# One row statistic of a state-space block, moved from GpSimd to ScalarE (Trainium2, one core)

## What is computed

```
def _layernorm(x, axis=-1, eps=1e-05):
    m = jnp.mean(x, axis=axis, keepdims=True)
    v = jnp.var(x, axis=axis, keepdims=True)
    return (x - m) / jnp.sqrt(v + eps)
...
    xz = einsum(hidden, in_proj_w);  x, z = halves of xz
    x_conv = silu(sum of 4 shifted x * conv_w + conv_b)
    dt_in, Bv, Cv = parts of einsum(x_conv, x_proj_w)
    delta = softplus(einsum(dt_in, dt_proj_w) + dt_proj_b)
    h = h * exp(d_t * A) + (d_t * u_t) * B_t;  y = sum over n of h * C_t
    y = (y + x_conv * D) * silu(z);  out = einsum(y, out_proj_w)
...
    x = x + _L0_attn_ref(_layernorm(x, axis=-1), ...)
    x = x + _L0_ffn_ref(_layernorm(x, axis=-1), ...)
```

## Time and profile before

| | |
|---|---|
| median of 3 runs | 6447.79 us (6447.11 to 6450.78) |
| the profiled execution, its own time | 6448.49 us |
| span of its profile | 6446.7 us |
| TensorE busy | 6085.9 us, 94% |
| GpSimd (POOL) busy | 5053.7 us, 78% |
| VectorE (DVE) busy | 4238.7 us, 66% |
| ScalarE (ACT) busy | 3553.7 us, 55% |
| granted TensorE clock, mean | 0.978 |

### The profile page before, as it was taken

One profiled execution on the slowest core, in us unless ns is written; L12 is line 12 of the kernel. 1 busy time (PEld: TensorE's weight loads), 2 busy tenths in 40 slices (PEclk: granted clock), 3 DMA queues, 4 the chain that ended last, 5 costly groups with the idle time before them and its releaser, 6 DMA issues. The chain is left out here.

```text
span 6446.7 us, 78759 instructions
## 1 busy us (share of the span) xinstructions
PE 6085.9 (94%) x25311; PEld 3902.1 (61%) x25312; DVE 4238.7 (66%) x5700; ACT 3553.7 (55%) x6456; POOL 5053.7 (78%) x3844
## 2 busy tenths in 40 slices
PE   7999999999999999999998699996999999999999
PEld 3444444444444444444443488885888888888887
DVE  6999999999999999999999567787000000000000
ACT  5677676767676776777676478873222222222221
POOL 6999999999999999999999687762445555554554
PEclk9999999999999999999999999998999999999999
DMA  3545554555555555555544334443666666666554
GB/s 122 165 164 170 165 171 162 164 168 168 165 164 172 165 166 166 170 162 165 170 166 161 99 100 124 124 128 72 180 183 181 189 185 180 189 186 179 178 169 123
DMA packets 562603, 1028.78 MB, mean 160 GB/s; under 512 B 90578, under 2 KB 256980, under 8 KB 527632
## 3 DMA queue, kind: packets, MB, share of 16 engines
q1 hardware_dynamic: 455088, 668.00, 32.6%
q0 software_dynamic: 107104, 355.74, 18.7%
HBM read 925.79 MB, written 88.08 MB: 157 GB/s over the span
## 5 line engine op out<-in xcount | busy, mean ns | idle before, releaser
L365 POOL TENSOR_TENSOR m_dbu<-m_du,m_bb 128x1024 f32<-128x1024 f32 x1024 | 2398.7, 2381 | 0.0
L743 PE MATMUL m_y_bank<-m_prod,m_ident 128*128 128x512 f32 x4096 | 1976.8, 612 | 147.3 <-POOL m_prod L374 147.3
L516 ACT ACTIVATE m_decay<-m_delta,m_a_neg 128x512 f32<-128x512 f32 x2048 | 1419.4, 695 | 725.7 <-DVE m_h L626 723.8
L743 PEld LDWEIGHTS m_y_bank<-m_prod,m_ident 128*128 128x128 f32 x4096 | 788.8, 196 | 1126.7 <-issue 907.5
L1795 DVE TENSOR_SCALAR e_ye<-e_ybank,e_share 128x256 f32<-128x256 f32 x270 | 118.2, 479 | 1768.3 <-PE e_ybank L1828 1768.3
L626 DVE TENSOR_TENSOR_SCAN m_h<-m_decay,m_h_end,m_dbu 128x512 f32<-128x512 f32 x1024 | 1258.5, 1265 | 3.6 <-ACT m_decay L516 2.5
L626 DVE TENSOR_TENSOR_SCAN m_h<-m_decay,m_dbu 128x512 f32<-128x512 f32 x1024 | 1196.2, 1204 | 12.6 <-ACT m_decay L516 12.0
L1776 ACT ACTIVATE e_a<-e_ubank 128x512 f32<-128x512 f32 x540 | 322.5, 597 | 1473.4 <-PE e_ubank L1819 1472.2
L374 POOL TENSOR_TENSOR m_prod<-m_h,m_cb 128x1024 f32<-128x1024 f32 x416 | 989.6, 2379 | 18.1 <-issue 13.7
L1819 PE MATMUL e_ubank<-e_xT,s_w 128*128 128x256 f32 x4320 | 978.4, 380 | 1.3 <-ACT e_xT L1767 1.3
L1828 PE MATMUL e_ybank<-s_w,e_a 128*128 128x256 f32 x4320 | 954.5, 379 | 0.7 <-ACT e_a L1776 0.7
(11 more groups left out here) (213 smaller groups left out, 6506.5 us busy)
## 6 DMA issues: line engine op xcount, KB each, us to landing
m_bb<-rows_bc SPq DMA_DIRECT2D x1024, 256.0 KB, 3.6
m_cv<-rows_bc SPq DMA_DIRECT2D x608, 256.0 KB, 3.8
m_cb<-rows_bc SPq DMA_DIRECT2D x416, 256.0 KB, 3.3
m_xin<-in_x SPq DMA_DIRECT2D x32, 512.0 KB, 5.6
m_xres<-in_x SPq DMA_DIRECT2D x32, 512.0 KB, 5.4
x<-m_xres SPq DMA_DIRECT2D x32, 512.0 KB, 6.0
a_xa<-x SPq DMA_DIRECT2D x64, 256.0 KB, 2.8
a_xr<-x SPq DMA_DIRECT2D x64, 256.0 KB, 3.2
```

Of the source, the lines that this page charges most:

```text
L365: nc.gpsimd.tensor_tensor(dbu[:, slot], du[:, q[1], p * PC:(p + 1) * PC], bb[:, slot].unsqueeze(1).to_broadcast([P, PC, T]), ALU.mult).the ...
L516: nc.scalar.activation(decay[:, cc], delta[:, r, c], ACT.Exp, scale=a_neg[:, c, n:n + 1]).then_inc(decay_done, 1)
L743: ins = nc.tensor.matmul(y_bank[:, cc], ident[:], prod[:, slot, cc], start=False, stop=(n == NS - 1))
```

## The change

GpSimd's four instructions and the two constants they read go. ScalarE gets a function of the same name with seven instructions: Ln of variance plus eps, Exp of minus half of that (the same inverse deviation), a multiplication by -1, and four one-column activations for -mean * rstd. The first three of them are each followed by a wait for their result. They are issued at v = 47, after the Exp of the second step-size group, and once ahead of the first block, where the table for Exp and Ln is loaded for them.

```
-            def inverse_deviation(q):
-                wait(pool, stats_done, count(q, 2, 2))
-                wait(pool, ln_done, count(q, 1, 0))
-                nc.gpsimd.tensor_tensor(rstd[:], moments[:, :, 1], eps[:], ALU.add).then_inc(rstd_done, 1)
-                nc.gpsimd.tensor_tensor(shift[:], moments[:, :, 0], minus_one[:], ALU.mult).then_inc(rstd_done, 1)
-                wait(pool, rstd_done, count(q, 4, 2))
-                nc.gpsimd.tensor_tensor(rstd[:], rstd[:], minus_half[:], ALU.pow).then_inc(rstd_done, 1)
-                wait(pool, rstd_done, count(q, 4, 3))
-                nc.gpsimd.tensor_tensor(shift[:], shift[:], rstd[:], ALU.mult).then_inc(rstd_done, 1)
...
-            inverse_deviation((0, 0))
-            inverse_deviation((0, 1))
...
-                        if u == STATS_AT // PC + 2 and not last:
-                            inverse_deviation(after(after(q)))
...
+            def inverse_deviation(q):
+
+                wait(act, stats_done, count(q, 2, 2))
+                wait(act, ln_done, count(q, 1, 0))
+                nc.scalar.activation(rstd[:], moments[:, :, 1], ACT.Ln, bias=eps[:, 0:1]).then_inc(rstd_done, 1)
+                wait(act, rstd_done, count(q, 4, 1))
+                nc.scalar.activation(rstd[:], rstd[:], ACT.Exp, scale=-0.5).then_inc(rstd_done, 1)
+                wait(act, rstd_done, count(q, 4, 2))
+                nc.scalar.mul(minus_rstd[:], rstd[:], -1.0).then_inc(rstd_done, 1)
+                wait(act, rstd_done, count(q, 4, 3))
+                for j in range(TB):
+                    ins = nc.scalar.activation(shift[:, j:j + 1], moments[:, j, 0:1], ACT.Identity,
+                                               scale=minus_rstd[:, j:j + 1])
+                ins.then_inc(rstd_done, 1)
...
+                if v == DEVIATE_AT and norm:
+                    inverse_deviation(after(q))
                 if v - NORMALISE_AT in (0, 1) and norm:
                     normalise(after(q), v - NORMALISE_AT)
...
+            nc.scalar.preload_act_table_set("natural_log_exp_and_others")
+            inverse_deviation((0, 0))
             normalise((0, 0), 0)
```

More of the change, by code:

```diff
@@ L104, in mamba_stage @@
     NORMALISE_AT = STATS_AT + 8
+    DEVIATE_AT = NORMALISE_AT - 2
     STORE_ROWS_AT = (position_of["dbl", 0] + 2 + TAKE) // PC
@@ L152, in mamba_stage @@
         shift = sb("shift", [P, TB])
-        minus_half = sb("minus_half", [P, TB])
-        minus_one = sb("minus_one", [P, TB])
+        minus_rstd = sb("minus_rstd", [P, TB])
         eps = sb("eps", [P, TB])
@@ L293, in _ @@
                 sp.dma_start(dst, src).then_inc(s_weights, 16)
-            sp.wait_ge(s_const, 5)
+            sp.wait_ge(s_const, 3)
             w_xT = w["x_T"].rearrange("(c p) e -> p c e", p=P)
@@ L334, in _ @@
         def _(pool):
-            nc.gpsimd.memset(minus_half[:], -0.5).then_inc(s_const, 1)
-            nc.gpsimd.memset(minus_one[:], -1.0).then_inc(s_const, 1)
             nc.gpsimd.memset(eps[:], EPS).then_inc(s_const, 1)
@@ L339, in _ @@
             nc.gpsimd.memset(w_x[:], 0.0).then_inc(s_const, 1)
-            pool.wait_ge(s_const, 5)
+            pool.wait_ge(s_const, 3)
             nc.gpsimd.affine_select(out=ident[:], in_=ident[:], compare_op=ALU.not_equal, fill=1.0,
                                     base=0, pattern=[[-1, P]], channel_multiplier=1).then_inc(s_const, 1)
-            def inverse_deviation(q):
-                wait(pool, stats_done, count(q, 2, 2))
-                wait(pool, ln_done, count(q, 1, 0))
-                nc.gpsimd.tensor_tensor(rstd[:], moments[:, :, 1], eps[:], ALU.add).then_inc(rstd_done, 1)
-                nc.gpsimd.tensor_tensor(shift[:], moments[:, :, 0], minus_one[:], ALU.mult).then_inc(rstd_done, 1)
-                wait(pool, rstd_done, count(q, 4, 2))
-                nc.gpsimd.tensor_tensor(rstd[:], rstd[:], minus_half[:], ALU.pow).then_inc(rstd_done, 1)
-                wait(pool, rstd_done, count(q, 4, 3))
-                nc.gpsimd.tensor_tensor(shift[:], shift[:], rstd[:], ALU.mult).then_inc(rstd_done, 1)
             def du_part(q, part):
@@ L406, in _ @@
             act.wait_ge(s_weights, 16 * 9)
-            act.wait_ge(s_const, 6)
+            act.wait_ge(s_const, 4)
             nc.scalar.activation(a_neg[:], a_log[:], ACT.Exp).then_inc(s_a, 1)
@@ L533, in _ @@
             dve.wait_ge(s_weights, 16 * 9)
-            dve.wait_ge(s_const, 6)
+            dve.wait_ge(s_const, 4)
             for c in range(CH):
@@ L657, in _ @@
             pe.wait_ge(s_a, 4)
-            pe.wait_ge(s_const, 6)
+            pe.wait_ge(s_const, 4)
             pe.wait_ge(s_weights, 16 * 9)
```

## The result

| | before | after |
|---|---|---|
| median | 6449.28 us (4 runs, 6447.11 to 6453.02) | 6498.8 us (4 runs, 6494.77 to 6506.6) |
| span of the profile | 6446.7 us | 6493.0 us |
| granted TensorE clock, mean | 0.978 | 0.974 |

The ratio is 1.0077, 95% interval 1.0065 to 1.0089: slower by 50 us, where 6457 us (between 6432 and 6478) had been forecast. The time went up by more than five times the forecast 9.6 us.

A forecast was written before the change was run, and what follows sets the result against it. GpSimd was taken as the bound, with VectorE close behind. The profiled 6448.5 us, plus 9.0 for 15 pairs and 0.6 at the start, gave 6458.1, stated as 6457 us against the runs' median; range 6432 to 6478 us.

The forecast's parts named there:

- What bounds the kernel: State-space stage: GpSimd, 99.4% busy, holds VectorE back by at most 1.12 us in one block and 1.36 in the other.
- The chain on ScalarE: Seven new instructions at v = 47: 1.6 us together, between 1.1 and 2.3 us.
- The dearer chain: Rival: ScalarE's seven instructions cost more than their pieces, deciding from about 1.7 us; 6478 us at 2.3 us; chance 0.21.
- the extra table load: Rival: a table load beside ScalarE's seven instructions in every block, 1.28 us x 30; excluded by the order of instructions.
- How late VectorE gets: Scans waiting for the decays of v = 48 and 50: VectorE 1.3 us late in even blocks, 1.55 in odd.
- the swap: GpSimd's four instructions against ScalarE's seven: one wait nearly replaces another, +0.18 us even block, +0.42 odd, +0.60 a pair.
- The second part of `m_du`: Odd block: GpSimd waits about 2 us for the last delta and starts 0.42 us later, delaying the gate by +0.42 us.
- A pair grows by 0.60 us, 15 pairs by 9.0 us: Sum over the loop: even block +0.18 us and odd block +0.42 us, times 15 pairs.
- TensorE's queue starts there from the gate. That wait moves with the gate and gives nothing back.: VectorE's 1.29 us wait after a gate, for ScalarE's C copy behind TensorE's fill: no gain from a shorter GpSimd.
- The start of the program: Ahead of the first block: +0.6 us from ScalarE's second preparation; two added table loads taken as costing 0.
- the signs that would show the prediction wrong: Profile after: small new waits for decays (faster), ScalarE's seven instructions over 1.8 us (slower), or unchanged waits at the gates.
- GpSimd's saving goes through: Rival: ScalarE delays no scan, so GpSimd's relief saves 37 us, to 6411 us; chance of a gain over 0.2%: 0.17.

## Why the prediction was wrong

- **What bounds the kernel.** Right in kind and in sum. "By no more" than 1.12 and 1.36 us a block does GpSimd hold VectorE back: that made 37 us for its four instructions. At full clock they cost 41 us, and the pair 2.45 us (221.15 - 218.70) against 2.48. That the sums agree so closely is in part luck, since the parts do not: at full clock the waits are 1.83 us in the even block and 0.31 in the odd. The 1.36 us of the odd block stood behind matmuls at the lower clock (3.45 us for four). Rows 3 also left out three waits of that pair, 0.34, 1.40 and 0.33 us; all three stand unchanged in the changed kernel, so nothing hangs on them.
- **The chain on ScalarE.** Right in length, 1.56 against 1.6 us. The dearer chain and the extra table load are out.
- **How late VectorE gets.** Even block 1.3 us forecast, 2.57 measured, but 0.98 at full clock. Odd block 1.55 forecast; 0.17 + 1.35 + 0.16 = 1.68 measured, but 0.15 at full clock, so that the forecast came near there by luck. Both sums rested on decays that the trace of before showed with little in hand. The odd block's were late there already (0.17 us), and at full clock that wait is gone: the four matmuls behind that block's v = 36 gate took 3.2 us in the trace of before and 1.98 with spare matmuls. The sign of the swap was wrong by this too: it was put at +0.60 us a pair and is -1.0.
- **The second part of `m_du`.** It was to start 0.42 us later from the gate; it starts 0.50 us later (36.60 against 36.10 us behind the gate at v = 36). GpSimd waits there for the last delta, as described, but 1.11, not 2 us, because it waits 1.09, 0.30 and 0.60 us ahead of its products before that. This agreement is luck as well: with the clock held, the multiplication starts 1.25 us *earlier* behind that gate than in the kernel before (34.90 against 36.15 us; its wait is 0.32 us), so the odd block's +0.42 us is no part of the swap.
- **The step that failed** is the sum "A pair grows by 0.60 us, 15 pairs by 9.0 us": it has no term for TensorE's own speed, and gives no reason for leaving it out. It goes back to "TensorE's queue starts there from the gate. That wait moves with the gate and gives nothing back." The wait itself did just that, and is still 1.29 us. But that step, and every sum behind it, took what TensorE does from the gates on as it stood in the trace: same matmuls, same durations, same distance to the fills that ScalarE takes. The matmuls took 3.67 for 1.98 us and 4.01 for 2.74, and ScalarE's fill came 1.7 us later. That was worth +4.4 us a pair, where my whole sum was +0.60.
- The rows were there to doubt it. In the earlier trace rows four matmuls take 3.45 us behind a wait of 2.97 us, where the same four take 1.88 us elsewhere in that trace (1032.00). I read the row for the wait and not for the duration beside it.
- **The start of the program.** The first matmuls behind a v = 4 gate start 1.2 us later (83.60 against 82.36), where 0.6 was put. The two added table loads cost nothing, as taken: ScalarE still waits 2.98 us for the statistics behind the first and 1.55 us for TensorE behind the second.
- **The rivals and the signs.** None was this one, and of the signs that would show the prediction wrong none came: the waits for decays were not small, the chain was not over 1.8 us, and the gates' waits shrank. The gain of "GpSimd's saving goes through" is real at full clock (no chain: 41 us below), but with the clock left to itself even the kernel without any chain won only 8 us.

The Trainium skill (TensorE: Matmul & The Clock Gate, What's actually happening) says that the low clock is the default and that activity releases it. The runs agree: spare matmuls in the waits bring the stage from 0.97 to 1.00.

What stays open is why a given wait loses the clock and another of the same length does not. The runs show that it depends on what lies around it (one covered wait changes the clock behind another), and no run here isolates more than that. Some 5.5 us of the 46.3 us between the spans lie outside the 15 pairs, 1.2 ahead of them and 4.3 behind, and were not followed up.

## What to carry to other kernels

When an engine that is nearly always busy has short waits, read the duration of the matmuls behind each wait and the granted clock there before costing anything: a change on other engines that moves those waits can move the clock, and it outweighed the change's own terms here by four to one. To judge a change by its own merit, compare both versions with spare matmuls in TensorE's waits. And if they bring the time down, keep them: they were worth 73 to 77 us to one version and 10 to the other. Then look again for the place of the moved work: two positions earlier it cost nothing here.

## What the hardware showed that I had not expected

- The same wait of 1.44 us ahead of the same matmuls keeps the clock in one pair of blocks (1.98 us at 580.67) and loses it in the next (3.65 us at 804.23), in one execution, and from then on in every pair to the last (3.65 to 3.68 us). In the kernel before it is the other way round: the first pair takes 3.67 us behind that wait (at 135.67), all later ones 1.98.
- Lengths of a pair gather at one value when the clock is not held: 221.88 us before, and in the profiled executions (each the slowest of ten) 221.86 without any chain and 221.87 with the chain at v = 45; 221.87 also in the changed kernel with spare matmuls at unit 1 alone. At full clock the first two differ by 2.45 us. In the kernel without any chain the saving was lost again behind waits at the lower clock; why the lengths meet at this value no run shows.
- More work was faster, twice: four more activations on ScalarE by 20 us, five spare matmuls a block on TensorE by 77 us.
- On ScalarE an instruction that waits for the result just before it starts 0.03 to 0.04 us after that one's end (1047.09 to 1047.12, 1047.32 to 1047.36), and four one-column activations with a pointer take 0.85 us together.
